# Down projection of the experts in seven products of halves, in a graph and attention layer on one core

## The chip, the cores and the metric

The kernel runs on one core of one Trainium2 chip. The metric is the device time of one execution in microseconds (us), the median of several runs. Engines: TensorE (PE; PEld is its weight load), VectorE (DVE), ScalarE (ACT), GpSimd (POOL), and SyncE (SP), which here only issues transfers. VectorE, ScalarE and TensorE reach PSUM, eight banks of 128 x 512 float32; GpSimd works in SBUF alone.

## The reference

```python
xn = layernorm(x)                                      # x: 1250 x 1024, 20000 edges
x = x + gnn(xn, edges, W, b) + linear_attention(xn, Wq, Wk, Wv, Wo, P)
y = layernorm(x)
weights = routing(y, Wr, temperature)                  # 1250 x 8
gate, up = y @ Wg[e], y @ Wu[e]                        # per expert e: 1024 x 128
h = silu(gate) * up
out = sum_e weights[:, e] * (h[:, e] @ Wd[e])          # Wd: 8 x 128 x 1024
return x + out
```

All in float32. The change lies in the last product. With `weights` multiplied into `h`, it is one matrix product of 1250 x 1024 hidden values (8 experts of 128) with a 1024 x 1024 matrix, added to `x`.

## The kernel before

Tokens are padded to 1280 (`NP`), ten tiles of 128 (`NT`). `KC` is 8 (blocks of 128 along the contraction), `W` is 512 (half of the output columns), a bank is 512 columns. Every float32 product is made of three in fp32r: each operand is split in a high part (a ScalarE copy rounds it) and a low part (raw less high, on VectorE or GpSimd), and TensorE adds high x high, high x low and low x high in one bank.

The expert stage makes the hidden values in 24 steps `n` (8 experts in 3 chunks of 512, 512 and 226 tokens); `expert(n, g)` gives gate and up with 24 matmuls each. ScalarE applies silu (`gate`), VectorE makes `product(n)` in two operations (up times the routing weight `wB`, L1543, then times silu, L1547), ScalarE copies it as high part (`hidden_high`, L1092) and GpSimd subtracts (`hidden_low`, L818). The low parts of the gate and up weights are GpSimd's too (`gu_low`).

The down projection has 20 tiles `d`: half `hf` of the columns and token tile `t`. `down(d, first, last)` puts 3 x 8 matmuls of 128 x 512 in one bank (L1938 to L1940); the first four tiles are made in two rounds, experts 0 to 3, then 4 to 7. Weight panels `d0` and `d1` (512 columns each) are loaded, rounded by ScalarE (L1046, 128x1024 pieces) and subtracted by GpSimd (L826). VectorE adds bank and `ob` (L1557), where `ob` holds four slots of `x` that SP loads from memory.

Every engine runs its own list in the order in which it is written, and waits on semaphores. SP's list for the outputs is:

```python
def load_o(d):
    ...
    if d >= 4:
        sp.wait_ge(o_st[d % 4], 16 * (d // 4))     # the slot's last store has landed
    sp.dma_start(ob[:, d % 4, :], ...)
...
for d in range(2 * NT):
    sp.wait_ge(d_dr, d + 1)
    sp.dma_start(out[t]..., ob[:, d % 4, :]).then_inc(o_st[d % 4], 16)      # L681
    if d + 4 < 2 * NT:
        load_o(d + 4)                                                       # L668
```

All transfers of this stage are in SP's one queue. The functions that the diff touches:

Of the kernel before, what the change touches and what calls it, by code (L numbers as in the profile page):

```python
# [15 lines left out]
P = 128  # L16
# [26 lines left out]
FIRST_WIN_STEP = NT + 1  # L43
CHUNKS = ((0, 512), (512, 1024), (1024, 1250))
# [60 lines left out]
def gps_layer(nc, x, src, dst, wk_nat, wq_nat, pbd, bk_col, bq_col, wv_pan, bv, wh_pan, bh, wo_t, bo,  # L105
              wgu_pan, wd_pan, wr_t, temp, out):
    ctx = ExitStack()
    with ctx:
# [3 lines left out]
        def sem(name):  # L112
            return ctx.enter_context(nc.semaphore(name))
# [102 lines left out]
        hTw = at("hTw", [P, 3, 2, NP], F32R, OW0)  # L216
        hT7 = at("hT7", [P, 2, NP], F32R, OS)
        sil = at("sil", [P, 2, W], F32, OS + 10240)
        prd = at("prd", [P, 2, W], F32, OS + 14336)
        wB = [at("wB0", [P, W], F32, OS + 18432), at("wB1", [P, W], F32, OW0 + 30720)]  # L220


        d0R = [at(f"d0R{k}", [P, 4, W], F32, OW1 + 8192 * k) for k in range(2)]
        d0L = [at(f"d0L{k}", [P, 4, W], F32R, OW1 + 8192 * k) for k in range(2)]
        d0H = [at(f"d0H{k}", [P, 4, W], F32R, OW1 + 16384 + 8192 * k) for k in range(2)]
        d1R = at("d1R", [P, KC, W], F32, OH)
        d1L = at("d1L", [P, KC, W], F32R, OH)
        d1H = at("d1H", [P, KC, W], F32R, OH + 16384)
        ob = at("ob", [P, 4, W], F32, OX + 20480)
# [7 lines left out]
        def hT(e):  # L237
            if e < 4:
                return xnH[:, e, :], xnL[:, e, :]
            return (hTw[:, e - 4, 0, :], hTw[:, e - 4, 1, :]) if e < 7 else (hT7[:, 0, :], hT7[:, 1, :])  # L240
# [13 lines left out]
        D_BANK = (0, 1, 5, 6, 2, 3, 4, 7)  # L254

# [28 lines left out]
        in_d = [sem(f"in_d{k}") for k in range(6)]  # L284
# [73 lines left out]
        hT_hi = sem("hT_hi")  # L358
        hT_lo = sem("hT_lo")
        d_hi = sem("d_hi")  # L360
        d_lo = sem("d_lo")
# [34 lines left out]
        def _(sp):  # L396
# [250 lines left out]
            def load_d0(k):  # L647
                sp.wait_ge(up_mm, 3 * (NEXP - 1 + k))
                sp.dma_start(d0R[k][:], wd_pan[0].rearrange("q (k n) -> q k n", n=W)[:, 4 * k:4 * k + 4, :])\
                  .then_inc(in_d[k], 16)  # L650
# [4 lines left out]
            for n in range(24):  # L655
                if n == 23:
                    load_d0(0)
                load_wb(n)
                e = n // 3
                if n % 3 == 2 and e + 2 < NEXP:  # L660
                    load_gu(e + 2)


            def load_o(d):
                hf, t = d // NT, d % NT
# [4 lines left out]
            load_d0(1)  # L670
# [4 lines left out]
            for piece in range(4):  # L675
                cols = slice(2 * piece, 2 * piece + 2)
                sp.dma_start(d1R[:, cols, :], wd_pan[1].rearrange("q (k n) -> q k n", n=W)[:, cols, :]).then_inc(in_d[2 + piece], 16)
            for d in range(2 * NT):
                hf, t = d // NT, d % NT
# [8 lines left out]
        def _(pool):  # L688
# [124 lines left out]
            def hidden_low(n):  # L813
                e, c = n // 3, n % 3
                first, last = CHUNKS[c]
                pool.wait_ge(hT_hi, n + 1)
                hi, lo = hT(e)
                pool.tensor_tensor(lo[:, first:last], prd[:, n % 2, 0:last - first], hi[:, first:last].bitcast(F32),  # L818
                                   ALU.subtract).then_inc(hT_lo, 1)

            def down_low(k):
                lo, raw, hi = ((d0L[0], d0R[0], d0H[0]), (d0L[1], d0R[1], d0H[1]), (d1L, d1R, d1H))[k]
                for piece in range((2, 2, 4)[k]):
                    cols = slice(2 * piece, 2 * piece + 2)
                    pool.wait_ge(d_hi, 2 * k + piece + 1)
                    pool.tensor_tensor(lo[:, cols, :], raw[:, cols, :], hi[:, cols, :].bitcast(F32), ALU.subtract)\  # L826
                        .then_inc(d_lo, 1)
# [3 lines left out]
            for n in range(24):  # L831
                e, c = n // 3, n % 3
                if c == 0:
                    pool.wait_ge(a_done, 2 * NT)
                    hi, lo = hT(e)
                    for m in (hi, lo):
                        pool.memset(m[:, N:NP].bitcast(F32), 0.0).then_inc(pads, 1)
                hidden_low(n)
                if c == 2 and e + 2 < NEXP:
                    gu_low(e + 2)  # L840
                if n == 21:
                    down_low(0)

            down_low(1)
            down_low(2)

        @block.scalar
        def _(act):
# [192 lines left out]
            def down_high(k):  # L1041
                hi, raw = ((d0H[0], d0R[0]), (d0H[1], d0R[1]), (d1H, d1R))[k]
                for piece in range((2, 2, 4)[k]):
                    cols = slice(2 * piece, 2 * piece + 2)
                    act.wait_ge(in_d[2 + piece if k == 2 else k], 16)
                    act.activation(hi[:, cols, :], raw[:, cols, :], ACT.Copy).then_inc(d_hi, 1)  # L1046

# [40 lines left out]
            def hidden_high(n):  # L1088
                e, c = n // 3, n % 3
                first, last = CHUNKS[c]  # L1090
                act.wait_ge(prod_step, 2 * n + 2)
                act.activation(hT(e)[0][:, first:last], prd[:, n % 2, 0:last - first], ACT.Copy).then_inc(hT_hi, 1)  # L1092
# [9 lines left out]
            for n in range(24):  # L1102
                e, c = n // 3, n % 3
                if n + 1 < 24:
                    gate(n + 1)
                hidden_high(n)
                if c == 2 and e + 2 < NEXP:
                    gu_high(e + 2)
                if n == 21:
                    down_high(0)  # L1110

            down_high(1)
            down_high(2)

        @block.vector
        def _(dve):
# [419 lines left out]
            def product(n):  # L1536
# [4 lines left out]
                if n >= 2:  # L1541
                    dve.wait_ge(hT_lo, n - 1)
# [4 lines left out]
                dve.tensor_tensor(prd[:, n % 2, 0:cols], prd[:, n % 2, 0:cols], sil[:, n % 2, 0:cols], ALU.mult)\  # L1547
                   .then_inc(prod_step, 1)

            for n in range(24):  # L1550
                product(n)


            for d in range(2 * NT):
                dve.wait_ge(in_o[d % 4], 16 * (d // 4 + 1))
                dve.wait_ge(d_mm, d + 1)
                dve.tensor_tensor(ob[:, d % 4, :], bank(D_BANK[d % 8]), ob[:, d % 4, :], ALU.add).then_inc(d_dr, 1)  # L1557

        @block.tensor
        def _(pe):  # L1560
# [355 lines left out]
            def down(d, first, last):  # L1916
                hf, t = d // NT, d % NT
                target, cols = bank(D_BANK[d % 8]), slice(t * P, (t + 1) * P)
                if first == 0:
                    if d >= 8:  # L1920
                        pe.wait_ge(d_dr, d - 7)
                    else:
                        pe.wait_ge(silu_done, 21 + d // 2)
                        pe.wait_ge(prod_step, 2 * (20 + d // 2) + 1)
                for e in range(first, last):
                    if d == 0 and e % 2 == 0:
                        pe.wait_ge(d_lo, e // 2 + 1)
                    if d == NT and e % 2 == 0:
                        pe.wait_ge(d_lo, 4 + e // 2 + 1)
                    if d < 4 and e % 4 == 3:  # L1930
                        pe.wait_ge(hT_lo, 12 if e < 4 else 24)
                        pe.wait_ge(hT_hi, 12 if e < 4 else 24)
                    hi, lo = hT(e)
                    if hf:
                        high, low = d1H[:, e, :], d1L[:, e, :]
                    else:
                        high, low = d0H[e // 4][:, e % 4, :], d0L[e // 4][:, e % 4, :]
                    pe.matmul(target, hi[:, cols], high, start=(e == 0), stop=False)  # L1938
                    pe.matmul(target, hi[:, cols], low, start=False, stop=False)  # L1939
                    mm = pe.matmul(target, lo[:, cols], high, start=False, stop=(e == KC - 1))  # L1940
                if last == KC:
                    mm.then_inc(d_mm, 1)

            pe.wait_ge(pads, 3 + 2 * NEXP)
            for d in range(4):
                down(d, 0, 4)
            for d in range(4):
                down(d, 4, KC)
            for d in range(4, 2 * NT):
                down(d, 0, KC)  # L1950
# [49 lines left out]
```

## Time and profile before

| what | value |
|---|---|
| median of 3 runs | 1101.61 us (1101.35 to 1101.86) |
| the profiled execution, its own time | 1102.07 us |
| span of its instructions | 1100.1 us |
| instructions | 15031 |
| TensorE busy | 1089.3 us, 99% |
| VectorE, ScalarE, GpSimd busy | 374.4, 251.4, 294.0 us |
| granted TensorE clock, mean | 1.00 of full speed |

The span goes from the first to the last instruction of the profiled execution. Busy is the time in which an engine had an instruction in work; matmuls overlap in their pipeline, so the distance from one to the next says more of TensorE's speed than the duration of one. Positions in the trace are us from the span's start.

### The profile page before, as it was taken

How to read it: one execution, taken by the hardware profiler on the slowest of the kernel's cores; microseconds unless marked ns; L12 is line 12 of the kernel's file. 1: busy time of each engine (PE TensorE's matmuls, PEld its weight loads, DVE VectorE, ACT ScalarE, POOL GpSimd, SP SyncE). 2: the span in 40 equal slices, each digit the busy share in tenths (PEclk: the TensorE clock that was granted, in tenths of full speed). 3: DMA queues.
4: the chain of work that ended last, by engine and by line, in shares of the span. 5: the costliest groups of instructions: out<-in, count | busy, mean ns of one | idle time of the engine just before them, and what ended most of it. 6: DMA issues, size and time to landing. Idle time of an engine off the chain costs nothing.

```text
span 1100.1 us, 15031 instructions
## 1 busy us (share of the span) xinstructions
PE 1089.3 (99%) x5647; PEld 903.7 (82%) x5647; DVE 374.4 (34%) x996; ACT 251.4 (23%) x398; POOL 294.0 (27%) x243
## 2 busy tenths in 40 slices
PE   8999999999999999999999999999999999999998
PEld 7887778887888888888788888887788888888887
DVE  6944656675631111322211223444321111111111
ACT  5320211121232344211111113334131111112000
POOL 4000011121141356300054445343142222235000
PEclk9999999999999999999999999999999999999999
DMA  7203012222243586504199987764032222215321
GB/s 266 96 29 106 13 35 59 67 70 67 66 146 119 188 287 218 187 1 153 42 277 322 292 234 204 232 190 140 1 87 62 62 62 62 74 59 212 115 96 67
DMA packets 145977, 139.28 MB, mean 127 GB/s; under 512 B 7958, under 2 KB 115826, under 8 KB 145650
## 3 DMA queue, kind: packets, MB, share of 16 engines
q1 hardware_dynamic: 145330, 136.48, 39.7%
q10 hardware_dynamic: 576, 1.84, 0.5%
q8 instruction: 47, 0.77, 0.3%
q14 instruction: 24, 0.20, 0.1%
HBM read 102.32 MB, written 35.96 MB: 126 GB/s over the span
## 4 chain that ended last, share of the span: by engine, by line
PE 95%; DVE 3%; DMA 1%; ACT 1%; issue 1%; SPq 0%; ACTq 0%; DVEq 0%
PE ps L1590 9%; PE ps L1592 9%; PE ps L1591 9%; PE ps L1890 7%; PE ps L1891 7%; PE ps L1892 7%; PE ps L1831 4%; PE ps L1825 4%; PE ps L1805 3%; PE ps L1756 3%; PE ps L1807 3%; PE ps L1806 3%; PE ps L1938 3%; PE ps L1939 3%; PE ps L1758 3%; PE ps L1940 3%
## 5 line engine op out<-in xcount | busy, mean ns | idle before, releaser
L1590 PE MATMUL ps<-w_hi,xnH 128*128 128x512 f32 x464 | 184.6, 398 | 0.0
L1592 PE MATMUL ps<-w_hi,xnL 128*128 128x512 f32 x464 | 180.9, 390 | 0.0
L1591 PE MATMUL ps<-w_lo,xnH 128*128 128x512 f32 x464 | 180.7, 389 | 0.0
L736 POOL TENSOR_TENSOR acc<-acc,cw 128x320 f32<-128x320 f32 x40 | 35.8, 894 | 252.6 <-ACT cw L920 251.5
L1590 PEld LDWEIGHTS ps<-w_hi,xnH 128*128 128x128 f32 x464 | 87.1, 188 | 18.7
L1592 PEld LDWEIGHTS ps<-w_hi,xnL 128*128 128x128 f32 x464 | 87.1, 188 | 18.5
L1591 PEld LDWEIGHTS ps<-w_lo,xnH 128*128 128x128 f32 x464 | 87.2, 188 | 17.2
L1543 DVE TENSOR_TENSOR prd<-ps,wB 128x512 f32<-128x512 f32 (+1 forms) x24 | 14.2, 592 | 161.9 <-PE ps L1892 147.8
L1756 PE MATMUL ps<-xnH,w_hi 128*128 128x512 f32 (+1 forms) x192 | 68.1, 355 | 0.0
L1890 PE MATMUL ps<-x2H,guH 128*128 128x512 f32 (+1 forms) x192 | 67.7, 352 | 0.4 <-ACT wT L1100 0.4
L1891 PE MATMUL ps<-x2L,guH 128*128 128x512 f32 (+1 forms) x192 | 67.6, 352 | 0.0
L1892 PE MATMUL ps<-x2H,guL 128*128 128x512 f32 (+1 forms) x192 | 67.5, 352 | 0.0
L1890 PE MATMUL ps<-xnH,guH 128*128 128x512 f32 (+1 forms) x192 | 67.5, 351 | 0.0
L1758 PE MATMUL ps<-xnH,w_lo 128*128 128x512 f32 (+1 forms) x192 | 67.4, 351 | 0.0
L1757 PE MATMUL ps<-xnL,w_hi 128*128 128x512 f32 (+1 forms) x192 | 67.4, 351 | 0.0
L1892 PE MATMUL ps<-xnH,guL 128*128 128x512 f32 (+1 forms) x192 | 67.4, 351 | 0.0
L1891 PE MATMUL ps<-xnL,guH 128*128 128x512 f32 (+1 forms) x192 | 67.3, 350 | 0.0
L1287 DVE TENSOR_SCALAR hot<-iota,key 128x128 f16<-128x128 f16 x179 | 55.5, 310 | 20.1 <-issue 18.3
L794 POOL TENSOR_TENSOR cL<-cR,cH 128x1280 fp32r<-128x1280 f32 x20 | 59.0, 2949 | 2.0 <-ACT cH L1014 1.4
L1288 DVE TENSOR_SCALAR hot<-iota,key 128x320 f16<-128x320 f16 x179 | 55.9, 312 | 0.2 <-issue 0.2
L1014 ACT ACTIVATE cH<-cR 128x1280 fp32r<-128x1280 f32 x20 | 25.5, 1276 | 99.3 <-POOL cR L789 99.0
L1557 DVE TENSOR_TENSOR ob<-ps,ob 128x512 f32<-128x512 f32 x20 | 13.8, 692 | 94.8 <-PE ps L1940 94.8
(316 smaller groups left out, 2068.7 us busy)
## 6 DMA issues: line engine op xcount, KB each, us to landing
cR<-c_d SPq DMA_DIRECT2D x20, 640.0 KB, 5.0
foldin<-in SPq DMA_DIRECT2D x32, 256.0 KB, 2.7
guR<-in SPq DMA_DIRECT2D x16, 512.0 KB, 5.4
w_raw<-in SPq DMA_DIRECT2D x14, 512.0 KB, 6.7
c_d<-cw SPq DMA_DIRECT2D x40, 160.0 KB
qs0H<-qT_d SPq DMA_DIRECT2D x10, 512.0 KB, 5.3
qs0L<-qT_d SPq DMA_DIRECT2D x10, 512.0 KB, 6.6
ob<-x_d SPq DMA_DIRECT2D x20, 256.0 KB, 2.7
```

What stands on the lines that cost most here:

```text
L794: pool.tensor_tensor(cL[k][:], cR[k][:], cH[k][:].bitcast(F32), ALU.subtract).then_inc(c_lo, 1)
L1287: dve.tensor_scalar(target1, iota[:, 0:P], key1[:, column], -512.0 * w, ALU.subtract, ALU.is_equal)
L1288: dve.tensor_scalar(target2, iota[:], key2[:, column], None, ALU.is_equal).then_inc(ready, 1)
L1590: pe.matmul(target, xnH[:, kc, cols], wH[w][:, kc, :], start=(kc == 0), stop=False)
L1591: pe.matmul(target, xnH[:, kc, cols], wL[w][:, kc, :], start=False, stop=False)
L1592: mm = pe.matmul(target, xnL[:, kc, cols], wH[w][:, kc, :], start=False, stop=(kc == KC - 1))
L1756: pe.matmul(target, wH[w][:, kc, block_cols], xnH[:, kc, first:last], start=(kc == 0), stop=False)
L1757: pe.matmul(target, wH[w][:, kc, block_cols], xnL[:, kc, first:last], start=False, stop=False)
L1758: mm = pe.matmul(target, wL[w][:, kc, block_cols], xnH[:, kc, first:last], start=False, stop=(kc == KC - 1))
L1890: pe.matmul(target, high, x2H(kc)[:, first:last], start=(kc == 0), stop=False)
L1891: pe.matmul(target, high, x2L(kc)[:, first:last], start=False, stop=False)
L1892: mm = pe.matmul(target, low, x2H(kc)[:, first:last], start=False, stop=(kc == KC - 1))
```

## The change

The contraction, the output columns and the token tiles are each cut in two. Token tiles r and r + 5 are the two halves of the rows (`HALF` = 5), experts 0 to 3 and 4 to 7 the halves of the contraction, 512 and 512 the halves of the columns. The 2 x 2 x 2 = 8 products of halves become seven, over sums and differences of halves (the form with seven products and 15 additions). A product q has 5 tiles r of 3 x 4 = 12 matmuls.

- Hidden values stay unsplit in float32 (`hT`); `hidden_high` and `hidden_low` go. For each of the 35 tiles ScalarE makes `token_high(i)` and VectorE `token_low(i)`, in rings of three (`hxH`, `hxL`), from `hT` or from sums of token halves.
- VectorE makes these sums: `first_sums(r)` (two operations), `third_sum(r)`, `fourth_sum(r)`, at fixed places of its loop over i.
- There are seven weight panels of 128 x 2048 each in place of two of 128 x 4096. VectorE makes panel 2 (`second_panel`, two operations of 128 x 2048), GpSimd panels 3 (one operation), 4 and 5 (four pieces of 128 x 512 each). ScalarE rounds each in one operation (`down_high`), GpSimd subtracts in four pieces (`down_low`), and TensorE waits for each piece (`wd_lo`).
- Partial results are joined in PSUM (products 0 and 1, 3 and 4, 5 and 6 share banks) and over SBUF (`u2`, `u3`: `first_product_out` on ScalarE, additions on VectorE). For results 5 to 19 GpSimd first adds `u2` or `u3` to `ob` (`add_earlier`), and VectorE's addition waits for it (`o_sum`). Results 0 to 4 come with product 1, 5 to 9 with product 4, 10 to 14 with 5, 15 to 19 with 6.
- SP loads panels 0 and 1 in the expert stage, two more after expert 6 and the last after expert 7. Its list for the outputs is as before; only the order of the tiles differs (`down_out`).

```diff
+        def hx_source(i):
+            q, r = divmod(i, HALF)
+            return (lambda: tokens(0, r), lambda: tokens(1, r), lambda: hs2[:, r], lambda: tokens(0, r + HALF),
+                    lambda: tokens(1, r + HALF), lambda: hs1[:, r], lambda: tokens(1, r))[q]()
...
+        def down_out(d):
+            return (0, d) if d < NT else (1, (d - HALF) % NT)
...
+            def down_low(q):
+                pool.wait_ge(wd_hi, q + 1)
+                for k in range(4):
+                    pool.tensor_tensor(wdL[q][:, k, :], wdR[q][:, k, :], wdH[q][:, k, :].bitcast(F32), ALU.subtract)\
+                        .then_inc(wd_lo, 1)
...
+            for e in range(2, NEXP):
+                gu_low(e)
+                if e in (4, 6):
+                    down_low((e - 4) // 2)
...
+            pool.wait_ge(in_d[2], 16)
+            pool.wait_ge(in_d[3], 16)
+            pool.tensor_tensor(wdR[3][:], wdR[6][:], wdR[3][:], ALU.subtract).then_inc(wd_mix, 1)
+            pool.wait_ge(wd_t2, 2)
             down_low(2)
+            pool.wait_ge(in_d[4], 16)
+            for k in range(4):
+                pool.tensor_tensor(wdR[4][:, k, :], wd_low_left[:, k, :], wdR[2][:, k, :], ALU.subtract).then_inc(wd_mix, 1)
+            down_low(3)
+            for k in range(4):
+                pool.tensor_tensor(wdR[5][:, k, :], wdR[6][:, k, :], wdR[2][:, k, :], ALU.subtract).then_inc(wd_mix, 1)
+            for q in range(4, 6):
+                down_low(q)
...
+            def add_earlier(d):
+                u, r = (u2, u3, u2)[d // HALF - 1], d % HALF
+                pool.wait_ge(in_o[d % 4], 16 * (d // 4 + 1))
+                pool.wait_ge(u_ok, (0, HALF, 0)[d // HALF - 1] + r + 1)
+                pool.tensor_tensor(ob[:, d % 4, :], ob[:, d % 4, :], u[:, r, :], ALU.add).then_inc(o_sum, 1)
+
+            for d in range(HALF, HALF + 3):
+                add_earlier(d)
+            down_low(6)
+            for d in range(HALF + 3, 2 * NT):
+                add_earlier(d)
...
+            for i in range(2, 7 * HALF):
+                token_high(i)
+                if 3 <= i < 3 + HALF:
+                    first_product_out(i - 3)
+                if i in (5, 7, 10, 13, 16):
+                    down_high({5: 2, 7: 3, 10: 4, 13: 5, 16: 6}[i])
...
+            def token_low(i):
+                dve.wait_ge(hx_hi, i + 1)
+                dve.tensor_tensor(hxL[i % 3][:], hx_source(i), hxH[i % 3][:].bitcast(F32), ALU.subtract)\
+                   .then_inc(hx_lo, 1)
...
+            for i in range(2, 7 * HALF + 3):
+                if i < 7 * HALF:
+                    token_low(i)
+                if i >= 3:
+                    product_out(i - 3)
+                if i in (2, 3):
+                    second_panel(i - 2)
+                if 4 <= i < 4 + HALF:
+                    first_sums(i - 4)
+                if 9 <= i < 9 + HALF:
+                    third_sum(i - 9)
+                if 18 <= i < 18 + HALF:
+                    fourth_sum(i - 18)
...
+            def down(q, r):
+                i, target = q * HALF + r, down_bank(GROUP[q], r)
+                bank_is_free(q, r)
+                pe.wait_ge(hx_lo, i + 1)
+                opens = q not in (1, 4, 6)
+                for k in range(4):
+                    if r == 0:
+                        pe.wait_ge(wd_lo, 4 * q + k + 1)
+                    hi, lo = hxH[i % 3][:, k, :], hxL[i % 3][:, k, :]
+                    high, low = wdH[q][:, k, :], wdL[q][:, k, :]
+                    pe.matmul(target, hi, high, start=(opens and k == 0), stop=False, skip_group_check=not opens)
+                    pe.matmul(target, hi, low, start=False, stop=False, skip_group_check=not opens)
+                    mm = pe.matmul(target, lo, high, start=False, stop=(k == 3), skip_group_check=not opens)
+                mm.then_inc(d_mm, 1)
```

`token_high(i)` waits until tile i - 3 is over (its slot of the ring is then free), and for the sum that it reads. `product_out(j)` is VectorE's part of tile j: nothing for product 0, results of products 1, 4, 5 and 6 (bank plus `ob`), `u2` and `u3` for products 2 and 3. 

## Rows read from the trace of the kernel before

**Rows 1.** The page, busy time of each engine and granted clock in 40 slices.
```profile
PE 1089.3 (99%) x5647; PEld 903.7 (82%) x5647; DVE 374.4 (34%) x996; ACT 251.4 (23%) x398; POOL 294.0 (27%) x243
...
PEclk9999999999999999999999999999999999999999
```

**Rows 2.** Chain that ended last, from 960 us on, its shares by line.
```profile
by line: PE ps L1938 25.8%; PE ps L1939 25.7%; PE ps L1940 25.7%; PE ps L1892 6.6%; PE ps L1891 6.6%; PE ps L1890 6.6%; DVE ob L1557 0.5%; issue 0.1%; DVEq L1556 0.0%
```

**Rows 3.** Windows: start and end, length, busy time (instructions) by engine, clock, DMA.
```profile
779.00:988.00 209.00, 208.64 (x1116) 179.48 (x1115) 40.29 (x97) 38.52 (x66) 62.01 (x54) 1.00 0.20 61
988.00:1097.00 109.00, 108.74 (x480) 89.69 (x478) 14.08 (x22) 6.65 (x7) 14.87 (x7) 1.00 0.35 123
```

**Rows 4.** Timeline, TensorE and VectorE: start, duration, instruction, [idle before, its releaser].
```profile
987.74 0.39 PE L1938 MATMUL ps<-d0H,xnH 128*128 128x512 f32 x1
...
1001.65 0.69 DVE L1557 TENSOR_TENSOR ob<-ps,ob 128x512 f32<-128x512 f32 x1 [12.77 <-PE ps L1940]
1004.37 0.69 DVE L1557 TENSOR_TENSOR ob<-ps,ob 128x512 f32<-128x512 f32 x1 [2.03 <-PE ps L1940]
...
1091.41 0.69 DVE L1557 TENSOR_TENSOR ob<-ps,ob 128x512 f32<-128x512 f32 x1 [4.75 <-PE ps L1940]
1096.85 0.69 DVE L1557 TENSOR_TENSOR ob<-ps,ob 128x512 f32<-128x512 f32 x1 [4.75 <-PE ps L1940]
```

**Rows 5.** Groups by line and shape: count, busy us, mean ns, idle before.
```profile
L1046 ACT ACTIVATE d0H<-d0R 128x1024 fp32r<-128x1024 f32 x4 | 4.0, 1050 | 3.5 <-DMA d0R<-in 3.5
L1092 ACT ACTIVATE hT<-prd 128x512 fp32r<-128x512 f32 x2 | 1.2, 623 | 0.0
...
L1333 DVE TENSOR_TENSOR w_lo<-w_raw,w_hi 128x1024 fp32r<-128x1024 f32 x4 | 4.9, 1214 | 0.0
```

**Rows 6.** Timeline, GpSimd and VectorE at the end of the expert stage.
```profile
978.34 1.30 POOL L818 TENSOR_TENSOR hT<-prd,hT 128x512 fp32r<-128x512 f32 x1 [10.33 <-ACT hT L1092]
979.59 4.74 POOL L826 TENSOR_TENSOR d0L<-d0R,d0H 128x1024 fp32r<-128x1024 f32 x2
...
983.43 1.44 DVE L1547 TENSOR_TENSOR prd<-prd,sil 128x512 f32<-128x512 f32 x1
```

**Rows 7.** Timeline, GpSimd and VectorE, 450 to 459 us.
```profile
450.02 8.03 POOL L701 TENSOR_TENSOR w_lo<-w_raw,w_hi 128x1024 fp32r<-128x1024 f32 x3 [9.40 <-ACT w_hi L874]
...
454.37 1.42 DVE L1396 SCALAR_TENSOR_TENSOR hL<-htmp,dis,hH 128x512 fp32r<-128x512 f32 x1 [0.79 <-ACT hH L998]
...
457.51 1.08 DVE L1396 SCALAR_TENSOR_TENSOR hL<-htmp,dis,hH 128x512 fp32r<-128x512 f32 x1 [0.79 <-ACT hH L998]
```

**Rows 8.** Timeline, VectorE and GpSimd, 321 to 324 us.
```profile
321.50 2.38 DVE L1363 TENSOR_TENSOR kvL<-kvF,kvH 128x512 fp32r<-128x512 f32 x2
...
321.57 1.75 POOL L742 TENSOR_TENSOR qL<-qF,qH 128x512 fp32r<-128x512 f32 x1
```

**Rows 9.** Timeline of SP's issues (L668 loads, L681 stores), and the stores' landing times.
```profile
1013.46 0.32 SPq L668 DMA_DIRECT2D ob<-x_d  x1
...
1017.22 0.32 SPq L668 DMA_DIRECT2D ob<-x_d  x1
...
1020.84 0.32 SPq L668 DMA_DIRECT2D ob<-x_d  x1
...
1024.47 0.32 SPq L668 DMA_DIRECT2D ob<-x_d  x1
1026.85 0.34 SPq L681 DMA_DIRECT2D out<-ob  x1
1028.89 0.32 SPq L668 DMA_DIRECT2D ob<-x_d  x1
...
DMA to landing us min/median/max: 2.0/2.0/5.0
```

**Rows 10.** DMA issues 1013.8 to 1017.4 (KB, us to landing), and GpSimd's addition by shape.
```profile
ob<-x_d SPq DMA_DIRECT2D x1, 256.0 KB, 2.9
...
L784 POOL TENSOR_TENSOR xh<-xh,bob 128x512 f32<-128x512 f32 x10 | 13.0, 1296 | 97.8 <-DMA bob<-in 95.0 <-DMA xh<-in 2.9
```

More of the change, by code:

```diff
@@ L254, in gps_layer, with down_bank @@
         D_BANK = (0, 1, 5, 6, 2, 3, 4, 7)
+        def down_bank(group, r):
+            return bank(D_BANK[(group * HALF + r) % 8])
         in_x = [sem(f"in_x{k}") for k in range(3)]
@@ L283, in gps_layer @@
         in_gu = [[sem(f"in_gu{k}_{g}") for g in range(2)] for k in range(2)]
-        in_d = [sem(f"in_d{k}") for k in range(6)]
+        in_d = [sem(f"in_d{k}") for k in range(5)]
         in_o = [sem(f"in_o{k}") for k in range(4)]
@@ L357, in gps_layer @@
         prod_step = sem("prod_step")
[L358 to L361, printed above, removed]
+        wd_mix = sem("wd_mix")
+        wd_t2 = sem("wd_t2")
+        wd_hi = sem("wd_hi")
+        wd_lo = sem("wd_lo")
+        hs = sem("hs")
+        hx_hi = sem("hx_hi")
+        hx_lo = sem("hx_lo")
+        p1_out = sem("p1_out")
+        u_ok = sem("u_ok")
+        o_sum = sem("o_sum")
         d_mm = sem("d_mm")
@@ L674, in _ @@
                 load_o(d)
-            for piece in range(4):
-                cols = slice(2 * piece, 2 * piece + 2)
-                sp.dma_start(d1R[:, cols, :], wd_pan[1].rearrange("q (k n) -> q k n", n=W)[:, cols, :]).then_inc(in_d[2 + piece], 16)
             for d in range(2 * NT):
-                hf, t = d // NT, d % NT
+                hf, t = down_out(d)
                 sp.wait_ge(d_dr, d + 1)
@@ L829, in _ @@
             for e in range(2):
                 gu_low(e)
[L831 to L842, printed above, removed]
@@ L844, in _ @@
-            down_low(1)
-            down_low(2)
+            pool.wait_ge(a_done, 2 * NT)
+            for k in range(2):
+                pool.memset(hT[k][:, :, N:NP], 0.0).then_inc(pads, 1)
+            for e in range(2, NEXP):
[5 more added lines that the diff above has]
+            pool.tensor_tensor(wdR[3][:], wdR[6][:], wdR[3][:], ALU.subtract).then_inc(wd_mix, 1)
@@ L1086, in gate, with down_high, token_high, first_product_out @@
                 act.activation(sil[:, n % 2, 0:cols], bank(PAIR[n % 4][0], cols), ACT.Silu).then_inc(silu_done, 1)
[L1088 to L1092, printed above, removed]
+            def down_high(q):
+                if q < 2:
+                    act.wait_ge(in_d[q], 16)
+                elif q == 2:
+                    act.wait_ge(wd_t2, 2)
+                elif q < 6:
+                    act.wait_ge(wd_mix, (1, 5, 9)[q - 3])
+                act.activation(wdH[q][:], wdR[q][:], ACT.Copy).then_inc(wd_hi, 1)
+            def token_high(i):
+                q, r = divmod(i, HALF)
+                if q == 0:
+                    act.wait_ge(prod_step, 24)
+                elif q in (1, 4):
+                    act.wait_ge(prod_step, 48)
+                    act.wait_ge(pads, 5)
+                else:
+                    act.wait_ge(hs, {2: 2 * r + 2, 3: 2 * HALF + r + 1, 5: 2 * r + 1, 6: 3 * HALF + r + 1}[q])
+                if i == 2:
+                    act.wait_ge(up_mm, 3 * NEXP)
+                if i >= 3:
+                    act.wait_ge(d_mm, i - 2)
+                act.activation(hxH[i % 3][:], hx_source(i), ACT.Copy).then_inc(hx_hi, 1)
+            def first_product_out(r):
+                act.wait_ge(d_mm, r + 1)
+                act.activation(u2[:, r, :], down_bank(0, r), ACT.Copy).then_inc(p1_out, 1)
             act.wait_ge(rt, 1)
@@ L1550, in _, with first_sums @@
             for n in range(24):
                 product(n)
[L1554 to L1557, printed above, removed]
+                if n in (21, 22):
+                    token_low(n - 21)
+            def first_sums(r):
+                dve.tensor_tensor(hs1[:, r], tokens(0, r + HALF), tokens(1, r + HALF), ALU.add).then_inc(hs, 1)
+                dve.wait_ge(hs, 2 * r + 1)
+                dve.tensor_tensor(hs2[:, r], hs1[:, r], tokens(0, r), ALU.subtract).then_inc(hs, 1)
@@ new lines, in third_sum, with fourth_sum, second_panel @@
+            def third_sum(r):
+                dve.tensor_tensor(tokens(0, r + HALF), tokens(0, r), tokens(0, r + HALF), ALU.subtract).then_inc(hs, 1)
+            def fourth_sum(r):
+                dve.tensor_tensor(tokens(1, r), tokens(1, r), hs2[:, r], ALU.subtract).then_inc(hs, 1)
+            def second_panel(step):
+                if step == 0:
+                    dve.wait_ge(up_mm, 3 * NEXP)
+                    dve.wait_ge(wd_mix, 1)
+                    dve.wait_ge(wd_lo, 4)
+                    dve.tensor_tensor(wdR[2][:], wdR[3][:], wdH[0][:].bitcast(F32), ALU.add).then_inc(wd_t2, 1)
+                else:
+                    dve.wait_ge(wd_t2, 1)
+                    dve.tensor_tensor(wdR[2][:], wdR[2][:], wdL[0][:].bitcast(F32), ALU.add).then_inc(wd_t2, 1)
@@ new lines, in result, with product_out @@
+            def result(d, group):
+                if d < HALF:
+                    dve.wait_ge(in_o[d % 4], 16 * (d // 4 + 1))
+                else:
+                    dve.wait_ge(o_sum, d - HALF + 1)
+                dve.tensor_tensor(ob[:, d % 4, :], down_bank(group, d % HALF), ob[:, d % 4, :], ALU.add).then_inc(d_dr, 1)
+            def product_out(j):
+                q, r = divmod(j, HALF)
+                if q == 0:
+                    return
+                dve.wait_ge(d_mm, j + 1)
+                if q == 1:
+                    result(r, 0)
+                elif q == 2:
+                    dve.wait_ge(p1_out, r + 1)
+                    dve.tensor_tensor(u2[:, r, :], down_bank(1, r), u2[:, r, :], ALU.add).then_inc(u_ok, 1)
+                elif q == 3:
+                    dve.wait_ge(u_ok, r + 1)
+                    dve.tensor_tensor(u3[:, r, :], down_bank(2, r), u2[:, r, :], ALU.add).then_inc(u_ok, 1)
+                else:
+                    result((q - 3) * HALF + r, (2, 3, 3)[q - 4])
@@ L1913, in _ @@
                     expert(n, g)
[L1916 to L1950, printed above, removed]
+            GROUP = (0, 0, 1, 2, 2, 3, 3)
+            def bank_is_free(q, r):
+                n = GROUP[q] * HALF + r
+                if q == 1:
+                    pe.wait_ge(p1_out, r + 1)
+                elif q == 4:
+                    pe.wait_ge(u_ok, HALF + r + 1)
+                elif q == 6:
+                    pe.wait_ge(d_dr, 2 * HALF + r + 1)
+                elif n < 8:
+                    pe.wait_ge(silu_done, 21 + n // 2)
+                    pe.wait_ge(prod_step, 2 * (20 + n // 2) + 1)
+                elif n - 8 < HALF:
+                    pe.wait_ge(d_dr, n - 8 + 1)
+                elif n - 8 < 2 * HALF:
+                    pe.wait_ge(u_ok, n - 8 - HALF + 1)
+                else:
+                    pe.wait_ge(d_dr, n - 8 - HALF + 1)
@@ L1954, in _panels @@
+            for q in range(7):
+                for r in range(HALF):
+                    down(q, r)
 def _panels(w, np):
```

96 lines of the change are left out of this document (45 added, 51 removed).

## Prediction

> **What bounds the kernel now.** I read the page's busy line first: TensorE is busy for 99% of the span at the full granted clock [rows 1]. The chain of waits from 960 us on then consists of its matmul lines, with half a percent of VectorE, the last result [rows 2]. The windows say the same of the two stages that the change touches: in the expert stage (779 to 988) and in the down projection (988 to 1097) TensorE has no idle time to speak of [rows 3]. So only fewer matmuls shorten this kernel, and anything that makes TensorE wait, or delays the last output behind its last matmul, lengthens it.
>
> The down projection starts with the matmul at 987.74; I count from there and call it 0. The 20 results follow each other by 5.44 us in the steady part; the first four, whose second halves of 12 matmuls end one after another, follow by 2.72 us [rows 4]: 0.2267 us each, no gap at a change of tile. The last result starts at 1096.85, which is 109.1. From there to the end of the span are 3.2 us (addition, store, landing), and they remain.
>
> **What is removed.** 20 tiles of 24 matmuls become 35 tiles of 12: 480 matmuls less 420 is 60, times 0.2267 is **13.6 us**. TensorE alone would end at 95.2. The split of the hidden values after every product (ScalarE copy, GpSimd subtraction) goes too; it lay beside a TensorE without idle time and gives nothing back.
>
> **What is added in the expert stage.** Two panel loads, two ScalarE copies of 128x2048 (2.0 us each, as twice 128x1024), eight GpSimd pieces of 1.25 us, and one GpSimd difference of 128x2048 (4.74 us, as its two halves) [rows 5, 6]. An expert lasts 27 us on TensorE, and each engine has some 10 us of this work in it at most. SP's loads of the last panels stand where one panel load stands now. Nothing of it is on the path: 0. If this cover were gone, the gate's or product's bank would be late, at most by one 4.7 us operation.
>
> **What is added in the down projection, per tile of 2.72 us.** ScalarE: a copy of 0.62. VectorE: `token_low`, a subtraction with both inputs in SBUF; from tile 5 on a result or `u2`/`u3` sum with one input in PSUM, 0.69; and `first_sums` (two more operations with both inputs in SBUF in steps 4 to 8), `third_sum` (one in 9 to 13), `fourth_sum` (one in 18 to 22). By duration alone that is 2.1 to 2.8 us per tile and could be borne. But GpSimd now has 24 pieces in a row for panels 2 to 5, and here the trace has a warning.
>
> VectorE's product at 983.43 took 1.44 us in place of 0.69: it ended 0.55 after the GpSimd operation that began at 979.59 and ended at 984.33 [rows 6]. At 454.37 and 457.51 it is the same with other tiles, and there GpSimd's three operations took 8.03 us where three of 2.38 are 7.1: each VectorE operation in between cost GpSimd some 0.45 [rows 7]. At 321.5 GpSimd's 128x512 piece took 1.75, again 0.46 over its 1.29, and VectorE's second operation waited until it was over [rows 8]. The addition from PSUM at 1001.65 ran in 0.69 amid GpSimd's pieces [rows 4]: it does not take part. So while GpSimd has pieces queued, both alternate, and each VectorE operation with two SBUF inputs costs a whole turn: 1.25 (spacing of GpSimd's 128x512, 978.34 to 979.59) plus 0.44, **1.69 us**. Operations from PSUM fit into GpSimd's part of the turn. The token operands are strided, four runs of 128 elements; no row shows that, and I take the contiguous price (bounds 0 and 0.1 more each).
>
> When does it start? Panel 2 is made in VectorE's steps 2 and 3 (two additions of 128x2048, 2.2 each by twice 1.21 less one start [rows 5]): the last product and `token_low(2)` end at 1.9, the first addition at 4.2, `token_low(3)` (tile 0 over at 3.0, ScalarE's copy at 3.6) at 4.9, the second addition at 7.1. ScalarE starts `token_high(5)` when tile 2 is over, at 8.4; with `first_product_out(2)` and `down_high(2)` (0.6, 0.6, 2.0) it is at 11.6. From 11.6 GpSimd works without a pause. `token_high(6)` ends at 12.2, GpSimd's first piece at 12.9, so `token_low(6)` at 13.3. From there to `token_low(14)` stand in VectorE's queue 8 `token_low`, 6 operations of `first_sums` and 5 of `third_sum`: 19 turns of 1.69 are 32.1, so the operand of tile 14 is ready at 45.4 (and 20 of the 24 pieces are used up, so the turns do last that long). TensorE restarts 0.25 later, at 45.7, and would have been there at 14 x 2.72 = 38.1: **7.5 us late**, taken from tile 8 on (some 2 us each at tiles 8 and 9, 0.65 each at 10 to 14). Bounds: 0 if the turns don't happen, 10 at 1.80 per turn. Afterwards one turn per tile fits, and the five double steps 18 to 22 (3.4 against 2.7) eat a lead of 3 us without a stall. TensorE ends at 102.7, 6.1 earlier than now. The panels' own `wd_lo` waits are no bound: panel 3's last piece falls at about 32, tile 15 starts at 48; panels 4 and 5 are later still.
>
> The Trainium skill, SBUF — State Buffer, "Who interferes with whom", says that a VectorE instruction with two SBUF inputs and a GpSimd instruction that reads SBUF exclude each other for the whole instruction; in these rows GpSimd gets on about 0.1 us before VectorE's end. By the page the turn would be 1.80 instead of 1.69, and the sum below 3.7 us higher.
>
> **The outputs.** From product 4 on each tile gives a result, every 2.72 us instead of 5.44. `ob` has four slots, and SP's queue is: wait for the result, store, wait for that store to land, load four results ahead. Behind that wait stands the next store. At the present pace a store lands 2.04 after its issue (1026.85 to 1028.89). Where results came at 2.72, the queue fell behind, and then the next store went out right behind each load: from load to load 3.76, 3.62 and 3.63 us (1013.46 to 1024.47) [rows 9]. A store that is behind a load lands later by about what the load still needs. So the queue's cycle is **3.66 us** against 2.72. Tile 20, which makes result 5, starts at 62.0 (45.7 and six tiles) and is over at 65.0; VectorE has `fourth_sum(4)` and `token_low(23)` ahead of the result, to 67.8, and the store is issued at 68.5. 2.04 later is the load for result 9, ten cycles later (36.6) the load for result 19, at 107.2. It lands 2.9 later [rows 10], GpSimd adds (1.29, and 0.1 of handing over), and the last result starts at **111.5**: 8.8 after TensorE's last matmul, where now it is 0.25. Results 13 to 16 wait up to 2.4 us for GpSimd's `o_sum` before that, but the operands of tiles 33 and 34 are ahead by about as much: no stall. Bounds: 0.25 behind TensorE if the queue keeps up; 3 us more if each cycle took 4.0, as one store that landed after 5.0 would make of some of them [rows 9].
>
> **Sum.** 60 matmuls -13.6, turns +7.5, outputs behind the last matmul +8.5: +2.4. The profiled execution's span is 1100.1 (its own time 1102.07, 0.46 above the median of the runs); 1102.5 is the new span, and 1101.61 + 2.4 = **1104.0** the median.
>
> **Rivals.**
> 1. *The outputs keep pace.* The load and the store behind it overlap once the pattern is steady, so the last result starts 0.25 after TensorE. For it: a store alone needs 2.04, less than a tile. Against it: the cycles just read, of the same two lines. Time: -13.6 + 7.5 = -6.1, **1095.5**. This is the rival on the faster side: all of it comes at a cycle of 2.8 or less (68.5 + 2.04 + ten cycles + 4.3 not past 103), and a cycle of 3.2 already makes the kernel faster by 0.2%. Chance 0.14.
> 2. *The turns cost little.* VectorE gets in between without waiting, or GpSimd's pieces are spread. For it: the port's turns are seen only in pairs here, never 19 in a row. Against it: in all the rows read the wait is whole. TensorE then ends at 95.2, result 5 comes some 9 us earlier, and only the outputs' queue is late by 6.8: -6.8, **1094.8**. Chance 0.12.
> 3. *Neither cost exists*, the change pays in full: -13.6, **1088.0**. Chance 0.03.
> 4. *A dearer turn*: the port is held to VectorE's end, or strided operands cost 0.1 more. 19 turns of 1.80 put TensorE 2.5 later and the double steps 1.2 more: +6.1, **1107.7**. Chance 0.14. The Trainium skill's page SBUF — State Buffer (section above) states the first of these.
> 5. *A part of one of the two costs*, for instance a cycle of 3.3, ten times 0.36 less: -1.2, **1100.4**. Chance 0.12.
>
> The forecast has 0.45, and its own range is 1100.5 to 1108, from a turn of 1.65 to 1.75 and a cycle of 3.6 to 3.9.
>
> **From these the numbers.** 0.2% (2.2 us) is about what a measurement of this kernel can tell from no change: below 1099.4 is faster, above 1103.8 slower. Faster: rivals 1 to 3, 0.29. Same: rival 5 and 0.4 of the forecast's weight, 0.30. Slower: the rest of the forecast and rival 4, 0.41. The range reaches over rivals 1 and 2 on the one side, and over rival 4 on the other: 1094.5 to 1108.5.
>
> **What the profile after would show.** 420 matmuls in the down projection, still 0.2267 apart inside a tile. `token_low` at 0.69 in the first five steps and 1.2 to 1.7 from about 13 to 60 us after the stage's start; TensorE idle before tiles 8 to 14, 7 us in all, released by VectorE's `hxL`. GpSimd's pieces 1.7 instead of 1.3. SP waiting for `out` to land in every cycle from result 5 on, the cycle near 3.66, and the last result 8 us after the last matmul. Wrong would be: `token_low` near 0.69 throughout (step: turns), store issues 2.72 apart at the end (step: outputs), or TensorE waiting for `wdL` (a panel late, which I cost at nothing). A lower granted clock in the gaps, which no row of before shows, would also spoil the sum.

## The result, and the profile after

| | before | after |
|---|---|---|
| median | 1101.59 us (10 runs, 1101.35 to 1101.86) | 1104.51 us (10 runs, 1103.89 to 1104.82) |
| ratio | | 1.0025, 95% interval 1.0016 to 1.0035 |
| span of the profiled execution | 1100.1 us | 1102.1 us |
| matmuls of the down projection | 480 | 420 |

The kernel became 2.9 us slower, 0.25%, with 60 matmuls fewer. In the profiled pair of executions the spans differ by 2.0. TensorE reaches its last matmul 6.1 us earlier than before; the last result starts 2.0 us later. The stage itself starts 0.3 us earlier in this profile (987.43) than in the one of before (987.74).

The page, first the lines that answer to [rows 1], then the shares of the chain that ended last by engine:

```profile
PE 1077.5 (98%) x5587; PEld 891.9 (81%) x5587; DVE 447.1 (41%) x1063; ACT 269.2 (24%) x413; POOL 331.3 (30%) x249
...
PEclk9999999999999999999999999999999999999998
...
PE 85%; POOL 6%; issue 4%; DVE 3%; ACT 1%; DMA 1%; POOLq 0%; SPq 0%; ACTq 0%; DVEq 0%
```

In the kernel before, the chain from 960 us on was TensorE's [rows 2]; now GpSimd has 6% of the whole span in it, and 4% are "issue", time for which the profile shows no instruction (here mostly transfers under way). The windows of the stage answer to [rows 3]:

```profile
988.00:1000.00 12.00, 12.00 (x55) 9.90 (x54) 10.68 (x13) 6.49 (x10) 1.02 (x1) 1.00 0.50 175
1000.00:1010.00 10.00, 9.40 (x42) 7.45 (x40) 9.93 (x7) 4.58 (x6) 10.00 (x7) 1.00 0.00 0
1010.00:1020.00 10.00, 6.21 (x25) 4.64 (x26) 9.97 (x9) 3.30 (x4) 10.00 (x7) 1.00 0.24 83
1020.00:1030.00 10.00, 8.86 (x37) 6.45 (x37) 10.00 (x10) 3.58 (x4) 10.00 (x7) 1.00 0.46 152
...
1092.00:1102.00 10.00, 0.00 (x0) 0.00 (x0) 1.38 (x2) 0.00 (x0) 2.52 (x2) 0.57 0.49 174
```

From 1000 to 1030 VectorE and GpSimd are both busy all the time and TensorE is not (25 matmuls in ten us where a full window has 44); and the last ten us have no matmul at all. These two stretches are the two costs. The first, in the timeline of VectorE, GpSimd and TensorE:

```profile
1004.16 1.78 DVE L1612 TENSOR_TENSOR hx1L<-hT,hx1H 128x512 fp32r<-128x512 f32 x1
1005.86 1.78 DVE L1622 TENSOR_TENSOR hs<-hT,hT 128x512 f32<-128x512 f32 x1
1007.68 1.67 DVE L1624 TENSOR_TENSOR hs<-hs,hT 128x512 f32<-128x512 f32 x1
1009.26 1.75 DVE L1612 TENSOR_TENSOR hx2L<-hT,hx2H 128x512 fp32r<-128x512 f32 x1
1010.94 0.68 DVE L1648 TENSOR_TENSOR ob<-ps,ob 128x512 f32<-128x512 f32 x1
...
1005.35 6.81 POOL L865 TENSOR_TENSOR wd4R<-wd_low_left,wd2R 128x512 f32<-128x512 f32 x4
...
1011.16 0.47 PE L2069 MATMUL ps<-wd1H,hx2H 128*128 128x512 f32 x1 [1.76 <-DVE hx2L L1612]
```

Each of these operations with two inputs in SBUF takes 1.7 to 1.8 us (1.2 where an addition from PSUM stands just ahead of it and fits into the same turn), the addition from PSUM 0.68, and four of GpSimd's pieces 6.81: 1.70 per turn. TensorE waits for `hx2L`, the low part that VectorE makes for tile 8. The second cost, in SP's issues (loads L698, stores L709), GpSimd's last addition and VectorE's last result:

```profile
1056.09 0.34 SPq L709 DMA_DIRECT2D out<-ob  x1
1058.10 0.32 SPq L698 DMA_DIRECT2D ob<-x_d  x1
1058.46 0.43 SPq L709 DMA_DIRECT2D out<-ob  x1
1061.72 0.32 SPq L698 DMA_DIRECT2D ob<-x_d  x1
...
1093.92 0.32 SPq L698 DMA_DIRECT2D ob<-x_d  x1
...
1097.15 1.26 POOL L877 TENSOR_TENSOR ob<-ob,u 128x512 f32<-128x512 f32 x1 [2.61 <-DMA ob<-x_d]
...
1098.87 0.69 DVE L1648 TENSOR_TENSOR ob<-ps,ob 128x512 f32<-128x512 f32 x1 [3.53 <-POOL ob L877]
```

The loads for results 9 to 19 go out from 1058.10 to 1093.92, ten cycles of 3.58 us, where tiles take 2.72. The last matmul starts at 1090.24, the last result 8.6 us after it (before: 0.5, 1096.36 to 1096.85 [rows 4]).

### The profile page after: what moved, and what is told of

Its sections match the earlier page's. It is cut to its first block, busy times and chain, and to the rows that moved or that the text cites. A ratio compares the mean times of both kernels' runs of the same rounds, so it can differ in the third digit from the quotient of the medians.

```text
span 1102.1 us, 15080 instructions
## 1 busy us (share of the span) xinstructions
PE 1077.5 (98%) x5587; PEld 891.9 (81%) x5587; DVE 447.1 (41%) x1063; ACT 269.2 (24%) x413; POOL 331.3 (30%) x249
## 4 chain that ended last, share of the span: by engine, by line
PE 85%; POOL 6%; issue 4%; DVE 3%; ACT 1%; DMA 1%; POOLq 0%; SPq 0%; ACTq 0%; DVEq 0%
PE ps L1713 9%; PE ps L1715 9%; PE ps L1714 9%; PE ps L2013 7%; PE ps L2014 7%; PE ps L2015 7%; PE ps L1954 4%; PE ps L1948 4%; PE ps L1928 3%; PE ps L1930 3%; PE ps L1929 3%; PE ps L1879 3%; PE ps L1881 3%; PE ps L1880 3%; PE ps L1723 2%
## 5 line engine op out<-in xcount | busy, mean ns | idle before, releaser
L764 POOL TENSOR_TENSOR acc<-acc,cw 128x320 f32<-128x320 f32 x40 | 35.8, 894 | 252.4 <-ACT cw L958 251.2
L838 POOL TENSOR_TENSOR guL<-guR,guH 128x1024 fp32r<-128x1024 f32 x16 | 38.0, 2399 | 144.6 <-ACT guH L1077 144.6
L1117 ACT ACTIVATE sil<-ps 128x512 f32<-128x512 f32 (+1 forms) x24 | 12.3, 519 | 154.6 <-PE ps L2015 149.0
```

## The experiments

All are edits of the changed kernel except where said; the ratio is to the kernel before.

### The load one store later

```diff
                 sp.dma_start(out[t][:, hf * W:(hf + 1) * W], ob[:, d % 4, :]).then_inc(o_st[d % 4], 16)
-                if d + 4 < 2 * NT:
-                    load_o(d + 4)
+                if d >= 1 and d + 3 < 2 * NT:
+                    load_o(d + 3)
```

> The changed kernel; SP issues the load for result d + 3 after the store of result d (it needs the store of d - 1, issued a tile earlier), in place of the load for d + 4, for which it had to wait until the store just issued had landed. Theory (SP's waiting list makes a cycle of 3.58 us against tiles of 2.72): the stores keep pace, the last result starts 0.3 us behind TensorE's last matmul in place of 8, TensorE's idle time stays at 7 us, so 1101.6 - 13.6 + 7.7 = 1095.7. Rival (the transfers themselves are too slow at this rate, whoever waits): the last result stays 6 us or more behind, 1102 or above.

Measured: **1095.74 us**, ratio 0.9947 (0.9930 to 0.9963). TensorE's last matmul starts at 1090.31, as in the changed kernel, and the last result 0.42 after it. SP waits 1.1 us in all for stores before it may load, where it waited 29.0 from 1050 on. The transfers themselves are fast enough; the order of the waits on SP cost 8.8 us. The rival falls.

### GpSimd's pieces replaced by writes that read nothing

```diff
-                pool.tensor_tensor(wdR[4][:, k, :], wd_low_left[:, k, :], wdR[2][:, k, :], ALU.subtract).then_inc(wd_mix, 1)
+                pool.memset(wdR[4][:, k, :], 0.0).then_inc(wd_mix, 1)
...
+                    if 2 <= q <= 5:
+                        pool.memset(wdL[q][:, k, :].bitcast(F32), 0.0).then_inc(wd_lo, 1)
+                        continue
```

(the same for panel 5's differences). Panels 4 and 5 are zero, and panels 2 and 3 lack their low part.

> The changed kernel; GpSimd's 24 pieces for panels 2 to 5 (differences and low parts) are replaced by writes of zeros to the same places, which read nothing from SBUF, so these panels are wrong or have no low part. Theory (turns between VectorE's operations with two SBUF inputs and GpSimd's reading pieces hold TensorE up): token_low stays at 0.7 us, TensorE idles less than 1 us in the down projection, and only the outputs' queue is late, by some 6: 1093.5 to 1095. Rival (VectorE is late by the number of its operations alone): TensorE still idles 7 us, 1104.

Measured: **1094.88 us**, ratio 0.9938 (0.9922 to 0.9955). VectorE has the same operations as in the changed kernel, and they are short again:

```profile
1001.99 0.69 DVE L1615 TENSOR_TENSOR hx1L<-hT,hx1H 128x512 fp32r<-128x512 f32 x1 [0.62 <-ACT hx1H L1144]
1002.60 0.69 DVE L1625 TENSOR_TENSOR hs<-hT,hT 128x512 f32<-128x512 f32 x1
1003.32 0.69 DVE L1627 TENSOR_TENSOR hs<-hs,hT 128x512 f32<-128x512 f32 x1
...
1000.79 1.93 POOL L868 MEMSET wd4R<- 128x512 f32 x4
```

The trace has no wait of TensorE in the down projection; its last matmul starts at 1082.41, 7.8 us earlier than in the changed kernel. So it is not the number of VectorE's operations. The zeros are also shorter (0.48 each) than the pieces. But if they took turns with VectorE, an operation beside them would last 0.48 + 0.44 = 0.92 (an estimate by the prediction's sum), and the one at 1001.99, with zeros being written until 1002.72, lasts 0.69: writes that read nothing take no part. The last result is at 1089.66, 7.2 after the last matmul: the outputs' queue, alone.

### Both

> Both edits together, with the same panels left out as in the run with zeros. Theory (there are these two costs and no third): the whole 13.6 us of the 60 matmuls, 1088.0. If something else holds (panel waits, waits per tile, bank reuse), 1090 or more.

Measured: **1087.98 us**, ratio 0.9874 (0.9857 to 0.9890). That is 13.6 us below 1101.6, the whole price of 60 matmuls, and the trace has no wait of TensorE for another engine. There is no third cost.

### Smaller and larger pieces

Each piece of GpSimd in two of 256 columns, with one count for both:

```diff
-                    pool.tensor_tensor(wdL[q][:, k, :], wdR[q][:, k, :], wdH[q][:, k, :].bitcast(F32), ALU.subtract)\
-                        .then_inc(wd_lo, 1)
+                    for c in (slice(0, 256), slice(256, 512)):
+                        low = pool.tensor_tensor(wdL[q][:, k, c], wdR[q][:, k, c], wdH[q][:, k, c].bitcast(F32), ALU.subtract)
+                    low.then_inc(wd_lo, 1)
```

> The changed kernel; each piece of GpSimd's down_low and of its differences is cut in two of 256 columns. Theory of turns: a turn falls from 1.70 to about 0.64 + 0.44 = 1.1 us, 19 of them are 21 us, so the operand of tile 14 is there before tile 13 ends: TensorE idles less than 1 us, result 5 comes some 8 us earlier, the outputs' queue is then the only cost: 1095 to 1096. Rival (port time adds up whatever the size of the pieces, with more fixed cost for more pieces): no better than 1104.5, GpSimd's panels late, TensorE waits for wd_lo.

Measured: **1105.94 us**, ratio 1.0037 (1.0023 to 1.0051). The expectation is missed by 10 us, though its first step holds: the turns are 1.1 us.

```profile
1003.64 1.22 DVE L1627 TENSOR_TENSOR hs<-hT,hT 128x512 f32<-128x512 f32 x1
1004.90 1.11 DVE L1629 TENSOR_TENSOR hs<-hs,hT 128x512 f32<-128x512 f32 x1
```

In its list of waits (us in total, times, longest) other lines have grown:

```profile
ACT wd5H L1131 <- POOL wd5R L872: 10.5, 1, 10.5
PEld ps L2074 <- issue: 8.4, 2, 5.9
PE ps L2074 <- DVE hx2L L1617: 7.6, 2, 5.5
...
ACT wd4H L1131 <- POOL wd4R L867: 6.1, 1, 6.1
```

ScalarE rounds panel 4 in its step 10 and panel 5 in its step 13, and there waits for GpSimd's differences; behind that wait stand the roundings of tokens 11 and 14, which VectorE and then TensorE need. In the changed kernel the same two waits were 2.1 and 2.3 us and lay beside VectorE's turns. Faster turns bring TensorE and ScalarE there sooner, and GpSimd, with twice the pieces, later: the differences of panels 4 and 5 end at 1016.2 and 1030.1, where they ended at 1012.2 and 1025.7. TensorE's clock fell to half behind the longest of these waits, which cost another 2.3 us (last section).

One operation per panel, in the other direction:

> The changed kernel; GpSimd's pieces for panels 2 to 6 are put together again, one operation of 128x2048 for each low part and each difference, and TensorE waits for the whole panel. Theory of turns: a turn is 4.7 + 0.44 us; three of them come between token_low(6) and token_low(7), so tile 7 starts 13 us late and some 2 more come later: 1108 to 1113. Rival (VectorE's own load sets TensorE's idle time): 1104 to 1105.

Measured: **1112.80 us**, ratio 1.0102 (1.0085 to 1.0119).

```profile
999.45 4.76 DVE L1613 TENSOR_TENSOR hx0L<-hT,hx0H 128x512 fp32r<-128x512 f32 x1 [0.79 <-ACT hx0H L1142]
1004.14 5.06 DVE L1623 TENSOR_TENSOR hs<-hT,hT 128x512 f32<-128x512 f32 x1
1009.23 4.87 DVE L1625 TENSOR_TENSOR hs<-hs,hT 128x512 f32<-128x512 f32 x1
1014.02 4.98 DVE L1613 TENSOR_TENSOR hx1L<-hT,hx1H 128x512 fp32r<-128x512 f32 x1
```

VectorE's 0.69 us operation takes 5, as long as GpSimd's, and TensorE stands for 11.8 us before tile 7. Behind that wait its matmuls are 0.427 us apart (half clock) from 1019.71 to 1024.40, which the expectation had not counted: TensorE ends 17.4 us late, where it had some 15. The turn follows the piece: 1.1, 1.7 and 5 us for 256, 512 and 2048 columns. So the time of a VectorE operation with two SBUF inputs is set by the length of the GpSimd operation beside it.

### Small pieces with ScalarE's panel roundings later

```diff
-                if i in (5, 7, 10, 13, 16):
-                    down_high({5: 2, 7: 3, 10: 4, 13: 5, 16: 6}[i])
+                if i in (5, 7, 12, 17, 19):
+                    down_high({5: 2, 7: 3, 12: 4, 17: 5, 19: 6}[i])
```

> The kernel with GpSimd's pieces of 256 columns, and ScalarE's roundings of panels 4, 5 and 6 moved from its steps 10, 13, 16 to 12, 17, 19. Theory (in the run with pieces of 256 ScalarE stood 6.1 and 10.5 us before GpSimd's differences, with the roundings of tokens 11 and 14 queued behind, and this took the gain): differences are made at 28.6 and 42.5 us after the stage's start, steps 12 and 17 come about there; TensorE idles less than 1 us, its clock does not fall, the last result waits for the outputs' queue alone: 1094.5 to 1096. Rival (the smaller pieces are dearer for VectorE or TensorE in themselves): 1102 or above.

Measured: **1099.62 us** (10 runs, 1098.75 to 1100.69), ratio 0.9979 (0.9969 to 0.9989). Half a hit. TensorE waits only some 2 us, its last matmul starts at 1084.71, 5.5 earlier than in the changed kernel, and its clock stays up. But the last result comes 10.9 after it. The queue starts late: result 5's store goes out at 1050.69, 63.0 after the stage's start (59.4 in the run with zeros), because GpSimd with twice the pieces reaches `add_earlier(5)` only at 1048.59. And in the profiled execution, the slowest of the ten (1100.69), one store took 5.26 us to land:

```profile
1066.91 0.32 SPq L698 DMA_DIRECT2D ob<-x_d  x1
1067.27 0.43 SPq L709 DMA_DIRECT2D out<-ob  x1
1072.53 0.32 SPq L698 DMA_DIRECT2D ob<-x_d  x1
```

> The same with the load order of the first run (load for result d + 3 behind the store of result d). Theory: nothing of the two costs is left with the work still on GpSimd: 1088.0 to 1089. Rival: more than 1090 if add_earlier, in GpSimd's turns with token_low, delays the results.

Measured: **1089.42 us**, ratio 0.9888 (0.9871 to 0.9904), 0.4 above the range. The 1.4 us over 1088.0 are TensorE's one wait of 1.1 for `hx0L` with its restart. With SP's order mended, GpSimd's later additions cost nothing.

> The changed kernel with pieces of 512 as they are and only the roundings of panels 4, 5 and 6 moved to ScalarE's steps 12, 17, 19. Theory (there VectorE's turns are the later of the two, the waits of 2.1 and 2.3 us on ScalarE lie beside them): no change, 1104 to 1105. Rival (these waits are a part of TensorE's 7 us): 1101 to 1103.

Measured: **1107.04 us**, ratio 1.0048 (1.0031 to 1.0064), against 1104.51: neither theory. TensorE ends almost as before the edit (last matmul at 1090.60, 0.4 later), so ScalarE's waits were indeed covered. But GpSimd now waits 6.3 us for panel 5's rounding, makes the rest of its list later, VectorE's double steps fall under its turns for longer, and result 5's store goes out at 1058.39 instead of 1056.09. The end is that store plus ten cycles, so those 2.3 us are most of the loss; the ten cycles took 36.4 us in place of 35.8 (1060.42 to 1096.77).

### The kernel before with the load one store later

> The kernel before with the load order of the first run. Theory (the queue costs only where results follow each other by less than its cycle of 3.6 us, and there they come every 5.44): the same, 1101.6 to 1101.8. Rival (the order is better in itself): faster by 1 us or more.

Measured: **1101.81 us**, ratio 1.0001 (0.9991 to 1.0010): no change, as both the profile of before, with VectorE waiting for TensorE alone, and the theory say. SP's order costs nothing at 5.44 us per result.

### VectorE makes the panels

```diff
+            pieces = [(kind, q, k) for kind, q in (("low", 2), ("low", 3), ("mix", 4), ("mix", 5), ("low", 4), ("low", 5),
+                                                   ("low", 6)) for k in range(4)]
+            per_step = {i: 1 for i in (*range(6, 14), *range(20, 29))}
+            per_step.update({i: 2 for i in range(14, 20)})
...
+                for _ in range(per_step.get(i, 0)):
+                    if pieces:
+                        panel_piece(*pieces.pop(0))
```

`panel_piece` is GpSimd's operation of 128x512 ("low": raw less high; "mix": the difference for panel 4 or 5) on VectorE, with the same waits; GpSimd's list loses them, and ScalarE's roundings of panels 4, 5, 6 stand in steps 16, 19, 22. SP's order is that of the first run.

> Whole computation. VectorE makes the panels 2 to 6 (their differences and low parts, 28 pieces of 128x512 at 0.6 us) between its token operations, one or two pieces per step; GpSimd keeps only the work of the expert stage and add_earlier; SP issues the loads one store later as in the first run. Theory: VectorE has 17 us more work in 95, no turns to wait for, TensorE does not idle: 1088 to 1090. Rival (VectorE becomes the bound by its busy time, up to 3.1 us in the steps 8 and 18 to 19, against 2.72): TensorE idles some us, 1091 to 1096.

Measured: **1088.06 us**, ratio 0.9876 (0.9859 to 0.9892), with the whole computation. The window from 988 to 1083:

```profile
988.00:1083.00 95.00, 95.00 (x420) 78.36 (x418) 80.23 (x114) 31.93 (x43) 21.21 (x15) 1.00 0.37 119
```

VectorE is busy for 80 of 95 us and TensorE has no gap. The turns are not quite gone, because GpSimd's `add_earlier` reads SBUF too: the pieces beside it took up to 1.8 us, the others 0.68, all 28 together 22.9, or 0.8 each, where a turn cost 1.7. The whole gain of the 60 matmuls is there. The last result starts 0.42 after the last matmul.

## Why the prediction was right

*Matmuls.* 13.6 us, from 0.2267 us for each of 60. The runs without the two costs lie 13.6 (1087.98) and 13.5 (1088.06) below the 1101.6 of before.

*Turns.* Forecast 1.69 us a turn and TensorE 7.5 us late; measured 1.70 and 7.8: from the stage's first matmul to its last are 102.8 us (987.43 to 1090.24), where 420 at 0.2267 make 95.0. At tile 14 it was 45.8 after the stage's start, forecast 45.7. TensorE's waits fell before tiles 8 to 14 and the trace names `hx0L`, `hx1L`, `hx2L`. The 0.1 that strided token operands might have cost did not appear: 4 turns at 6.81 us. The run with zeros shows that the turns are the cause, the three sizes of pieces that a turn is as long as the piece. By the Trainium skill's page SBUF — State Buffer, "Who interferes with whom", which the prediction cites (exclusion "for the whole instruction"), I had estimated 1.80; the measurement decides for 1.70: GpSimd goes on about 0.1 before VectorE's record ends. The price I put on that rival is also a little high: 19 turns at 0.11 more are 2.1 us, not 2.5.

*Outputs.* Forecast: store of result 5 at 68.5 after the stage's start, cycle 3.66, last result 8.5 further behind the last matmul than before. Measured: 68.7 (1056.09 less 987.43), 3.58, 8.1. The last result starts 111.4 after the stage's start, forecast 111.5, and that it is so close is partly luck. The store of result 5 was 0.2 later; ten cycles were 0.8 shorter, as the average of three cycles of before was 0.08 too long; GpSimd's last addition starts 3.2 after the load's issue (1093.92 to 1097.15), not 2.9; and from its start to the last result are 1.7 us, not 1.4. One reading was wrong: a store behind a load does not land later "by about what the load still needs". It landed 3.3 us after its issue (1058.46 to 1061.72), 1.25 later than a store alone, while the load, landing after 2.9 in the median, still needed some 2.5. The sum did not use that sentence, only the cycles. The order of the waits on SP, and not the transfers, is shown as the cause by the first run.

*Sum.* +2.4 forecast, +2.0 in the spans of the profiled executions, +2.9 in the medians. The last two differ by which executions were profiled: the one of before (1102.07) is 0.5 above its median, the one of the changed kernel (1103.89) is the fastest of its ten, 0.6 below the median. Why executions of one kernel differ is not shown. Two things could have a part. A store that takes 5 us in place of 3.3, seen once in the kernel before and once in a run with small pieces, lengthens this kernel in full. And the three executions of the changed kernel with a mean granted clock of 0.993 or 0.994 have spans of 1102.8 to 1103.0 us, the seven with 0.995 or 0.996 have 1102.1 to 1102.7. The lower end of the forecast's own range, 1100.5, does not come out of its terms either: a turn of 1.65 and a cycle of 3.6 give 1102.6.

*Rivals.* The outputs keeping pace (1095.5) and the turns costing nothing (1094.8) each came out as an experiment, at 1095.74 and 1094.88: the arithmetic held for the worlds that did not come to pass too.

*What I costed at nothing and had not weighed.* "The panels' own waits are no bound" was true, but only for TensorE's `wd_lo` waits. ScalarE's two waits for GpSimd's differences, with token roundings behind them, were covered by the turns alone, and the run with small pieces, where I again left them out, shows what they cost when the cover goes. Nor had I named as a lever how early result 5 comes; the run with only ScalarE's roundings moved shows it: TensorE's end stays, the kernel's moves by 2.5.

## What to carry to other kernels

Fewer matmuls pay only if the engines that feed and drain TensorE stay inside its new, shorter tile, counted with what they do to each other: take the price of a VectorE operation with two SBUF inputs from a moment in which GpSimd was reading too. When a tile gets shorter, look at every list in which an engine waits for its own transfer to land before it issues the next; here moving one load behind the next store was worth 8.8 us, and nothing at all at the old rate. And work that was moved to an idle engine may be cheaper on the busy one: 28 pieces more on VectorE, at 0.8 us on the average, gave back what GpSimd's cost at 1.7 beside it (1095.7 to 1088.1 us).

## What the runs showed of the hardware that I had not expected

TensorE's granted clock fell to half after a wait of 5.5 us, in the run with pieces of 256. The windows around tile 14:

```profile
1032.00:1034.00 2.00, 0.42 (x1) 0.45 (x2) 1.37 (x3) 2.00 (x5) 2.00 (x4) 0.50 0.00 0
1034.00:1036.00 2.00, 2.00 (x6) 1.52 (x6) 2.00 (x5) 1.44 (x1) 2.00 (x3) 0.50 0.00 0
1036.00:1038.00 2.00, 2.00 (x7) 1.52 (x6) 0.43 (x1) 0.00 (x0) 2.00 (x4) 0.50 0.00 0
...
1040.00:1042.00 2.00, 2.00 (x11) 1.64 (x10) 1.04 (x2) 0.29 (x1) 2.00 (x3) 1.00 0.00 0
```

The 12 matmuls of the tile are 0.427 us apart (1034.14, 1034.57, 1035.00) instead of 0.227, 1.2 GHz instead of 2.4, which made the wait 2.3 us dearer. The same happened behind the wait of 11.8 us in the run with one operation per panel.

But a long wait is not needed. In the run with only ScalarE's roundings moved, TensorE waited 1.75 and 2.07 us before tiles 8 and 9, and its clock was at half for most of tile 9:

```profile
1016.32 0.47 PE L2069 MATMUL ps<-wd1H,hx0H 128*128 128x512 f32 x1 [2.07 <-DVE hx0L L1612]
...
1016.00:1018.00 2.00, 1.69 (x5) 1.42 (x6) 2.00 (x4) 0.00 (x0) 2.00 (x2) 0.70 0.19 71
1018.00:1020.00 2.00, 2.00 (x6) 1.54 (x6) 2.00 (x2) 0.00 (x0) 2.00 (x2) 0.50 0.25 80
```

In the profiled execution of the changed kernel the waits before the same tiles were 1.76 and 2.11 us, and the clock stayed at 1.00 until the matmuls ended. So the length of the wait before a tile does not decide it alone; what does is not shown. In this place it cost nothing, as VectorE's turns were later than TensorE anyway: tile 12 starts at 1026.50, in the run with only the load moved, at full clock, at 1026.51.

VectorE and GpSimd take strict turns when both have a queue of work that reads two inputs from SBUF: in the 40 us from 999 to 1039 the 24 pieces of GpSimd and 23 operations of VectorE with both inputs in SBUF alternate one by one. And a store issued 0.4 us behind a load in SP's queue lands after some 3.2 us instead of 2.0.
